# A cross-attention and coupling network on one core: GpSimd's finished batches one slot sooner, and two tanhs moved into the end of the feed-forward stage

## The reference, cut to what matters

```python
x = x + attention(layernorm(x), ctx, ctx, mask, W_out)   # 16 heads of 16 features
    # u = q k^T * scale / 4;  logits = tanh(u) * exp(log_C);  softmax over the keys;  @ W_out.T
h = layernorm(x)
gf = global_net(mean of h over the tokens)               # per batch: 256 -> 128 -> 64 -> 1
out = h
for _ in range(3):
    tf = coupling_net(out)                               # per token: 256 -> 256 -> 128 -> 64 -> 1, exact gelu
    out = out + (0.1 + range * (0.7 * gf + 0.3 * tf - 0.5) * 2) * twist(out)
x = x + out                                              # twist swaps and negates quarters of the features
```

## Time and profile before

| | |
|---|---|
| time, median of 3 runs (lowest to highest) | 1145.98 us (1143.54 to 1146.03) |
| the profiled execution: its own time | 1144.29 us |
| its span, from the first to the last instruction | 1142.4 us |
| mean granted TensorE clock | 0.976 |
| PE busy | 988.3 us (87%) |
| ACT busy | 925.6 us (81%) |
| DVE busy | 815.8 us (71%) |
| POOL busy | 627.6 us (55%) |

### The profile page before, as it was taken

One profiled execution on the slowest core, in us unless ns is written; L12 is line 12 of the kernel. 1 busy time (PEld: TensorE's weight loads), 2 busy tenths in 40 slices (PEclk: granted clock), 3 DMA queues, 4 the chain that ended last, 5 costly groups with the idle time before them and its releaser, 6 DMA issues.

```text
span 1142.4 us, 21970 instructions
## 1 busy us (share of the span) xinstructions
PE 988.3 (87%) x7260; PEld 533.2 (47%) x7260; DVE 815.8 (71%) x1738; ACT 925.6 (81%) x1153; POOL 627.6 (55%) x1117
## 2 busy tenths in 40 slices
PE   6889989889888998889988898888988889886893
PEld 4555435544454434544355443554435544353431
DVE  4887577866687586885858859588586876777285
ACT  4999679987799877997779977899778996795576
POOL 4577306992179802897048960499405993068204
PEclk8999999999999999999999999999999999998897
DMA  4111001210022100220002200122001210001002
GB/s 121 54 43 32 1 2 65 72 49 1 1 72 66 47 0 2 92 69 24 1 26 77 70 14 2 46 71 69 0 2 56 70 60 1 1 29 38 10 1 75
DMA packets 67280, 43.85 MB, mean 38 GB/s; under 512 B 42080, under 2 KB 50784, under 8 KB 67168
## 3 DMA queue, kind: packets, MB, share of 16 engines
q1 hardware_dynamic: 67168, 42.45, 13.2%
HBM read 25.51 MB, written 16.78 MB: 37 GB/s over the span
## 4 chain that ended last, share of the span: by engine, by line
PE 31%; DVE 23%; POOL 17%; ACT 14%; issue 14%; DVEq 0%; DMA 0%; POOLq 0%; ACTq 0%; SPq 0%
PE ps L1190 7%; PE ps L1177 7%; ACT probs L882 6%; PE ps L1203 5%; DVE move_u L770 4%; ACT probs L888 3%; PE ps L1114 3%; POOL f_hat L452 3%; POOL rstd L442 2%; POOL xy L516 2%; DVE coup L736 2%; DVE f_t L774 2%; PE ps L1233 2%; DVE move_u L749 2%; DVE o_n L692 2%
## 5 line engine op out<-in xcount | busy, mean ns | idle before, releaser
L882 ACT ACTIVATE probs<-ps,u_scale 120x2048 f32<-120x2048 f32 x128 | 254.4, 1987 | 26.8 <-PE ps L1114 26.7
L888 ACT ACTIVATE probs<-probs,exp_bias,clip 120x2048 f32<-120x2048 f32 x128 | 270.9, 2117 | 0.1
L1203 PE MATMUL ps<-h,w 128*128 128x512 f32 x384 | 184.2, 605 | 14.4 <-ACT h L914 13.6
L1114 PE MATMUL ps<-q_t,k_t 32*120 32x256 f32 x2048 | 150.7, 408 | 42.3 <-ACT probs L882 41.4
L471 POOL TENSOR_TENSOR c<-tok_c 128x16 f32<-128x16 f32 x8 | 1.8, 224 | 320.6 <-issue 320.6
L1145 PE MATMUL ps<-wo_t,of_t 128*128 128x256 f32 x512 | 147.5, 412 | 3.3 <-DVE xy L705 3.3
L1130 PE MATMUL ps<-probs,va 120*32 120x256 f32 x2048 | 139.6, 391 | 4.7 <-ACT probs L888 4.6
L680 DVE STREAM_TRANSPOSE o_t<-ps 128x512 f32<-128x512 f32 x128 | 90.2, 705 | 65.4 <-PE ps L1130 65.1
L1114 PEld LDWEIGHTS ps<-q_t,k_t 32*120 32x120 f32 x2048 | 94.9, 182 | 71.1 <-issue 66.4
L1145 PEld LDWEIGHTS ps<-wo_t,of_t 128*128 128x128 f32 x512 | 88.9, 193 | 58.8 <-issue 47.6
L1203 PEld LDWEIGHTS ps<-h,w 128*128 128x128 f32 x384 | 66.8, 188 | 89.9 <-issue 64.8
(11 more groups left out here) (129 smaller groups left out, 1848.9 us busy)
## 6 DMA issues: line engine op xcount, KB each, us to landing
xy<-in_x_dram SPq DMA_DIRECT2D x64, 256.0 KB, 2.7
out_dram<-xy SPq DMA_DIRECT2D x64, 256.0 KB, 2.0
cbuf<-in_ctx_dram SPq DMA_DIRECT2D x64, 120.0 KB, 2.5
tok_c<-coup SPq DMA_DIRECT2D x256, 0.5 KB, 2.0
move_v<-in_L_xattn_W_out_dram SPq DMA_DIRECT2D x1, 256.0 KB, 5.5
move_u<-in_L_ffn_cn_w_dram SPq DMA_DIRECT2D x1, 256.0 KB, 5.7
w<-in_L_ffn_cn_w_dram SPq DMA_DIRECT2D x1, 128.0 KB, 5.7
g<-in_L_ffn_gc_w_dram SPq DMA_DIRECT2D x1, 128.0 KB, 4.1
```

Source lines behind the costliest of these rows:

```text
L882: eng.activation(probs[:, b % 2, n * HALF:(n + 1) * HALF, :].rearrange("k h q -> k (h q)"), banks(SCORE_BANK, 4)[0:KEYS, :], ACT.Tanh, sca ...
L888: eng.activation(p, p, ACT.Exp, scale=clip[0:KEYS, 0:1], bias=exp_bias[:, b:b + 1]).then_inc(s_exp, 1)
L1114: last = eng.matmul(banks(SCORE_BANK + r)[0:KEYS, odd * S:(odd + 1) * S], k_t[rows, b % 2, odd, n, :], q_t[rows, b % 2, n, :], start=True, ...
L1203: last = eng.matmul(banks(bank), w2[:, k, :], h1[:, p % 2, k, :], start=(k == 0), stop=(k == EK - 1))
```

## The change

GpSimd's list: in every slot `query_scale(new)` now comes between `norm_2_scale` and `norm_2`, and the old batch's two parts come together behind `norm_2`; slot 0 handles two old batches, so that each further slot handles a batch one slot sooner and slot 7 has none. In slot 0 `coefficients` still follow `norm_2`. VectorE's list is unchanged.

ScalarE's list: both tanhs of slot 0 move into the feed-forward stage, behind `gelu3(9)` and behind `gelu3(10)`; slot 0 begins with its exp. TensorE's list: `scores(early, 0)` behind `layer3(9)`, `scores(early, 1)` behind `layer3(10)`, `weighted_values(early - 1, 0)` behind `layer3(11)`; slot 0 is then `project(old, 0)`, `queries`, `weighted_values(here, 1)`, `keys`, `project(old, 1)`, `norm_to_features`.

```diff
@@ gpsimd
-                if after_ffn(i):
-                    if i - LAG < NB:
-                        norm_2_scale(i - LAG)
-                        norm_2(i - LAG)
-                    coefficients(groups_before(i) - 1)
-                for b in late[:1]:
-                    twisted_part(b)
-                if 0 <= i - LAG < NB and not after_ffn(i):
+                if 0 <= i - LAG < NB:
                     norm_2_scale(i - LAG)
-                for b in late[:1]:
-                    x_part(b)
-                late = late[1:]
-                if 0 <= i - LAG < NB and not after_ffn(i):
-                    norm_2(i - LAG)
                 if new is not None and 2 <= new < NB:
                     query_scale(new)
+                if 0 <= i - LAG < NB:
+                    norm_2(i - LAG)
+                if after_ffn(i):
+                    coefficients(groups_before(i) - 1)
+                for b in late[:2] if after_ffn(i) else late[:1]:
+                    twisted_part(b)
+                    x_part(b)
+                late = late[2:] if after_ffn(i) else late[1:]
                 if 0 <= i + 1 < NB:
                     values(i + 1)
@@ scalar
-                    if 0 <= i < NB:
+                    if 0 <= i < NB and not first:
                         tanh(i, 0)
                     if 0 <= i - 1 < NB and not first:
                         exp(i - 1, 1)
+                    if 0 <= i < NB and not first:
+                        tanh(i, 1)
                     if 0 <= i < NB:
-                        tanh(i, 1)
                         exp(i, 0)
...
+                    early = i * GROUP + GROUP + LAG
...
                             gelu3(i, p - 1)
+                            if early < NB and p >= PASSES - 2 and p < PASSES:
+                                tanh(early, p - PASSES + 2)
@@ tensor
-                    if 0 <= i < NB and i != early:
-                        scores(i, 0)
...
+                    if i != early:
+                        (scores, weighted values, queries, scores, project as before)
+                    else:
+                        if old < NB:
+                            project(old, 0)
+                        if nxt < NB:
+                            queries(nxt)
+                        if here < NB:
+                            weighted_values(here, 1)
                     if 0 <= nxt < NB:
                         keys(nxt)
-                    if 0 <= here < NB:
+                    if 0 <= here < NB and i != early:
                         weighted_values(here, 1)
...
-                        if p == PASSES and early < NB:
-                            scores(early, 0)
...
+                        if early < NB:
+                            if p == PASSES - 2:
+                                scores(early, 0)
+                            if p == PASSES - 1:
+                                scores(early, 1)
+                            if p == PASSES:
+                                weighted_values(early - 1, 0)
```

More of the change, by code:

```diff
@@ L1267, in _ @@
                         largest_spread()
-                    if 0 <= i < NB and i != early:
-                        scores(i, 0)
-                    if 0 <= here < NB:
[L1271 to L1277, removed]
+                    if i != early:
+                        if 0 <= i < NB:
+                            scores(i, 0)
+                        if 0 <= here < NB:
+                            weighted_values(here, 0)
+                        if 0 <= nxt < NB:
+                            queries(nxt)
+                        if 0 <= i < NB:
+                            scores(i, 1)
+                        if 0 <= old < NB:
+                            project(old, 0)
+                    else:
+                        if old < NB:
+                            project(old, 0)
+                        if nxt < NB:
+                            queries(nxt)
+                        if here < NB:
+                            weighted_values(here, 1)
                     if 0 <= nxt < NB:
                         keys(nxt)
-                    if 0 <= here < NB:
+                    if 0 <= here < NB and i != early:
                         weighted_values(here, 1)
```

## The result

The changed kernel takes 1112.8 us, the median of four runs (1110.33 to 1115.15), against 1144.76 for the kernel before beside it: ratio 0.9724, 95% interval 0.9694 to 0.9755. The forecast was 1109.4. The profiled execution took 1110.33, 1108.5 of them its span, 33.9 less than the span before. A second measurement on another occasion gave 1111.29, ratio 0.9712 (0.9696 to 0.9728).

A forecast was written before the change was run, and what follows sets the result against it. Bounds: GpSimd's crowded list in slots 4 to 7 and ScalarE's waits in slot 0. Terms 16.1 + 15.0 + 3.8 = 34.9 us off 1144.29 gave 1109.4, range 1100 to 1127 us for 8 in 10.

The forecast's parts named there:

- boundary, less what is given back: Feed-forward end into slot 0: slot 1 begins 2.6 us sooner, 0.3 given back; 2.3 us times 7, 16.1 us.
- GpSimd's list, slots 4 to 7: An old batch's parts leave the crowded slots for slot 0: 2.5 us a turn, times 6, 15.0 us.
- last attention stage: Slots 5 to 7 without queries, a loop through GpSimd and VectorE: 3.8 us gained, bounds 0 and 5.7.
- first attention stage: No old batches there; `norm_2` 4.75 to 5.85 us into the slot, under 6.65: set at 0.
- `norm_2` late in slot 2: Sign against the forecast: `norm_2` late already in slots 2 and 3; it must be over by 6.65 us.
- the 9.24 and the 9.7: GpSimd's forecast slot length in us: 9.24 with `norm_2` at 1.10, 9.7 with it at 1.53.
- The query hat: TensorE's queries wait for it 0.5 us in slot 6, 1.1 in slot 7; over 1.5 would speak against the forecast.
- The rule: GpSimd and VectorE ports lock for a whole instruction: each slot some 0.25 us longer, sum about 7 smaller, 1117 us.
- GpSimd stays as crowded: Rival: slots 4 to 7 keep their 36.8 us, leaving the boundary and some last stage; 1127 us, chance 0.15.
- The boundary gives nothing: Rival: TensorE's slot 0 list stays as late, the last gelu slipping 3 us, not 1.4; 1125.5 us, chance 0.08.
- Slower: Rival: every large GpSimd instruction in slots 2 to 7 meets VectorE, 12.2 us a slot; 1182 us, chance 0.05.
- No effect: Rival: tanhs wait as long for late scores, old batch only swaps with `query_scale`; within 0.3%, 1144 us, chance 0.02.

The follow-up runs named there:

- GpSimd's list alone: Only the GpSimd part of the change, ScalarE's and TensorE's lists as before, against the kernel before: 1130.52 us, ratio 0.9888.
- `query_scale` behind: The changed kernel with `query_scale` put behind `norm_2` again, old batches still behind both: 1115.22 us, ratio 0.9751 to the kernel before.
- two slots of two: The changed kernel with two old batches in slot 1 as well, so slots 6 and 7 have none: 1110.15 us, ratio 0.9707 to the kernel before.
- the query hat first: The changed kernel with values and query hat ahead of the old batch's two parts: 1106.9 us, ratio 0.9678 to the kernel before.

## Why the prediction was right

The terms, from the two profiled executions (us, seven boundaries and six turns):

| step | forecast | measured |
|---|---|---|
| boundary, less what is given back | 16.1 | 16.4 |
| GpSimd's list, slots 4 to 7 | 15.0 | 14.2 |
| last attention stage | 3.8 | 1.8 |
| first attention stage | 0 | -0.4 |
| the rest: longer turns of the kernel before (0.9 and 1.4), feed-forward stages (-0.4) | not in it | 1.9 |
| sum | 34.9 | 33.9 |

The four terms that were forecast come to 32.0, which is also the difference of the medians. That the profiled spans come nearer to 34.9 is luck: two turns of the kernel before lay longer in that execution, where its clock fell.

- **Boundary: right, and by its mechanism.** `gelu3(9)` to slot 1 fell by 18.7 us over seven boundaries (104.64 to 85.96). 0.9 of that is the first turn before (15.75), where the clock fell, and 0.2 is given back in slots 1 to 4 of each of the six full turns (25.34 to 25.40 against 25.16), 1.4 with the last. That leaves 16.4. TensorE ends last, as the step had it. The 0.2 is near the 0.3 of the step, but reaches TensorE by another way than the keys. In slot 2 VectorE's chain comes 0.33 us later against ScalarE than with GpSimd's list alone, where nothing is lost. `query_scale` waits 0.85 us for the statistics, its small instructions then fall on `combine` and the float16 copy, `norm_2` ends 6.76 us into the slot, over the 6.65 of the prediction, and TensorE's transposes wait 0.21 for it. So one more sign against it, `norm_2` late in slot 2, came true at a small price. With `query_scale` behind, the slots take 25.17.
- **GpSimd's list: the mechanism right, the nearness of the total luck.** Its lengths held: `norm_2` at 1.09, the values at 0.86, one long instruction of 1.63; the slot came to 9.43, between the 9.24 and the 9.7. With TensorE at full clock slot 4 to the end is 33.88, 2.9 us less than before, inside 2.3 to 3.8; six times that is 17.3, 2.3 more than was taken. Three turns gave back 3.5, a loss that the prediction did not have: 2.9 to the lower clock and 0.6 to the fifth turn's longer slots 4 to 6. (The remaining 0.4 are two longer turns before.) The sum of 9.24 holds a slip of 0.02: by its rows the query hat is 1.06, not 1.08.
- **The query hat: this sign came out wrong.** The step gave waits of 0.5 and 1.1 us in slots 6 and 7 and named more than 1.5 as a mark against it; they are 1.76 and 1.86. Alone they cost little, since moving the query hat forward left slot 4 to the end at 33.85. Their cost is the clock that falls behind them in some turns.
- **The last stage: mis-sized.** Forecast 3.8, measured 28.65 - 26.90 = 1.8, and 2.7 with the kernel repeated; with GpSimd's list alone it was 3.6. In both profiles of the changed kernel VectorE's division lay beside GpSimd's parts once (1.94 and 1.87 us instead of 0.69), and in the first TensorE also ran at half clock after it (0.75 from 1008 to 1012 us). From one transposes to the next this slot takes 8.37 us with both, 7.42 with the long division at full clock, and 6.41 with neither (GpSimd's list alone), so each cost about 1 us. The prediction had neither. The first profile, VectorE and then GpSimd:

```profile
1006.69 1.94 DVE L688 TENSOR_TENSOR o_n<-o_t,inv_sum 128x512 f32<-128x512 f32 x1
```

```profile
1005.86 1.10 POOL L516 TENSOR_SCALAR xy<-xy,x_fac,x_add 128x256 f32<-128x256 f32 x2
1006.92 1.17 POOL L525 TENSOR_TENSOR f_hl<-f_t,f_hl 128x512 f16<-128x512 f32 x1
```

- **The rule.** The division takes some 0.7 us in 34 of its 64 places; here 1.94, 1.25 more, about the 1.17 of the GpSimd instruction that ran beside it. The trace agrees with the Trainium skill (SBUF — State Buffer, "SBUF: two separate sides"): one of the two waits for the whole of the other's instruction, and it can be VectorE as well as GpSimd. The prediction's estimate of 1117 by that rule came out too high all the same: it added a collision to each slot, while the order took others away. Its own row was read too narrowly: beside the `norm_2` of 2.05 us VectorE ran `combine` as well as the float16 copy, so the 0.95 is the price of both. The costliest groups of GpSimd's lines over the changed kernel's span (busy us, mean ns of one) show both:

```profile
L507 POOL TENSOR_SCALAR twisted<-xy,neg,b_r 128x256 f32<-128x256 f32 x112 | 77.9, 707 | 1.2 <-POOL x_add L471 1.1
L452 POOL TENSOR_SCALAR f_hat<-xy,neg,rstd 128x256 f32<-128x256 f32 x128 | 74.7, 592 | 5.4 <-POOL rstd L442 5.4
...
L432 POOL TENSOR_SCALAR va<-cbuf 120x256 f32<-120x256 f32 x64 | 56.2, 877 | 0.0
```

Before, the means were 596, 828 and 1062 ns: the twisted parts became 12 us longer in all, `norm_2` and the values 42 us shorter.

- **The rivals.** GpSimd stays as crowded: no, 9.43 a slot and 33.9 instead of 36.8. The boundary gives nothing: no, 12.15. Slower: no, GpSimd's slot stayed under the 10.5 us where it turns. No effect: no.

## What to carry to other kernels

On a crowded engine, put a short independent instruction between the one that makes a value and the large one that reads it, and see what the large one then meets on the other engine: `query_scale` ahead of `norm_2` was worth 1.1 us a turn (1.3 less 0.2) though it delays `norm_2`. When a list is reordered, look at what TensorE waits for next, even where removing the wait alone gains nothing: after a rest of under 2 us inside a dense stretch it can run at half clock. And reckon two edits together where one hides the other's cost; here they gave 2 us more than the sum by the profiled executions, 5 by the medians.

## What the runs showed of the hardware

- The clock level behind a rest was not fixed. After waits of 1.7 to 1.9 us for the query hat the granted clock fell to its lower level in 18 of 26 turns (the changed kernel twice, GpSimd's list alone, two slots of two, and two turns with `query_scale` behind). After waits of 2.3 to 2.4 us, in the four other turns with `query_scale` behind, it didn't fall. With the rest filled or the query hat first, it fell in slots 6 and 7 in none of 24. Which of the turns fall is open.
- Eight transposes that compute nothing (1.09 us of TensorE's time in a wait) took the lower clock out of these slots in all twelve turns of two kernels. The times came out some 3 us lower (ratios 0.9724 and 0.9712 to 0.9689, and 0.9707 to 0.9678), but the intervals overlap, so the gain in time is not shown beyond doubt.
- Collisions of GpSimd and VectorE hit both engines and instructions of any size: a division of 0.69 us took 1.94 beside a GpSimd instruction of 1.17, a twisted part of 1.10 took 1.63 beside a division of 0.69, and a tiny GpSimd instruction of 0.23 took 0.47 beside an addition of 0.41. Whether they meet changes from turn to turn of one execution.
